# Sums over partitions in batches of eight steps through a ring of twelve products, and all fields gathered into one ring

## What is computed

```
e = jnp.stack([tbl_0[ids[:, 0]], ..., tbl_39[ids[:, 39]]], axis=1)      # 2048 x 40 x 64
vi, vj = e[:, i_idx, :], e[:, j_idx, :]                                  # 780 pairs i < j
viW = jnp.einsum('bpd,pde->bpe', vi, W)
z = jnp.einsum('bpe,bpe->bp', viW, vj)                                   # 2048 x 780
h = jnp.concatenate([z, dense_ctx], axis=1)
h = jnp.maximum(h @ W_top1 + b_top1, 0.0)                                # 796 -> 512
h = jnp.maximum(h @ W_top2 + b_top2, 0.0)                                # 512 -> 256
y = h @ W_top3                                                           # 256 -> 1
```

## Time and profile before

| | |
|---|---|
| median of 3 runs | 1378.1 us (1376.8 to 1378.47) |
| the profiled execution: its time | 1377.84 us |
| its span, first to last instruction | 1376.0 us |
| granted TensorE clock, mean | 0.994 |
| PE busy | 1305.7 us, 95% of the span, 7024 matmul records |
| DVE busy | 926.0 us, 67% |
| POOL busy | 605.2 us, 44% |
| ACT busy | 77.8 us, 6% |

### The profile page before, as it was taken

One profiled execution on the slowest core, in us unless ns is written; L12 is line 12 of the kernel. 1 busy time (PEld: TensorE's weight loads), 2 busy tenths in 40 slices (PEclk: granted clock), 3 DMA queues, 4 the chain that ended last, 5 costly groups with the idle time before them and its releaser, 6 DMA issues.

```text
span 1376.0 us, 16855 instructions
## 1 busy us (share of the span) xinstructions
PE 1305.7 (95%) x7024; PEld 463.0 (34%) x7024; DVE 926.0 (67%) x803; ACT 77.8 (6%) x97; POOL 605.2 (44%) x647
## 2 busy tenths in 40 slices
PE   1389999999999999999999999999999999999998
PEld 0133333333333333333333333333333333333333
DVE  0257888888656567787765666788776566788860
ACT  0000000000000000000000000000000000000001
POOL 6766443266754355766655456667660000000000
PEclk9989999999999999999999999999999999999999
DMA  4122221222222222222222223223221111111001
GB/s 151 26 62 62 57 70 52 68 61 65 82 54 68 66 72 75 62 82 63 63 59 82 63 66 87 61 62 83 63 62 52 52 54 52 53 44 54 1 1 42
DMA packets 36180, 84.43 MB, mean 61 GB/s; under 512 B 12420, under 2 KB 12420, under 8 KB 36104
## 3 DMA queue, kind: packets, MB, share of 16 engines
q1 hardware_dynamic: 11520, 52.43, 11.4%
q0 software_dynamic: 20560, 21.34, 7.9%
q10 hardware_dynamic: 4024, 9.58, 2.3%
HBM read 83.30 MB, written 0.01 MB: 61 GB/s over the span
## 4 chain that ended last, share of the span: by engine, by line
PE 92%; POOL 4%; issue 2%; DMA 1%; ACT 0%; DVE 0%; DVEq 0%; POOLq 0%
PE u L497 52%; PE zacc L512 27%; PE tacc L552 7%; PE u L471 3%; POOL gathered L312 2%; POOL first_fields L312 2%; PE tacc L555 2%; PE u L552 1%; DMA index<-ids 1%; PE u L555 1%; DMA gathered<-tbl,index 1%; PE tacc L559 1%; ACT h L369 0%; DVE prod L429 0%; DVEq L204 0%
## 5 line engine op out<-in xcount | busy, mean ns | idle before, releaser
L429 DVE TENSOR_TENSOR prod<-u,emb 128x1024 f32<-128x1024 f32 x800 | 925.8, 1216 | 409.2 <-PE u L497 409.2
L497 PE MATMUL u<-emb,weights 64*128 64x512 f32 x3200 | 753.6, 608 | 1.2 <-ACT emb L338 1.2
L312 POOL DMA_INDIRECT gathered<-tbl,index x512 | 482.9, 943 | 361.2 <-DVE prod L429 221.0
L497 PEld LDWEIGHTS u<-emb,weights 64*128 64x128 f32 x3200 | 291.6, 187 | 433.0 <-DVE prod L429 210.7
L512 PE MATMUL zacc<-prod,band 128*32 128x512 f32 x3200 | 391.7, 598 | 1.6 <-DVE prod L429 1.6
L512 PEld LDWEIGHTS zacc<-prod,band 128*32 128x32 f32 x3200 | 85.2, 109 | 278.9 <-DVE prod L429 147.9
L312 POOL DMA_INDIRECT first_fields<-tbl,index x128 | 120.8, 944 | 63.4 <-issue 32.6
L552 PE MATMUL tacc<-z,w12s 128*128 128x512 f32 (+1 forms) x196 | 97.4, 618 | 4.7 <-ACT h L369 4.7
L338 ACT ACTIVATE emb<-u 128x1024 f32<-128x1024 f32 x40 | 40.9, 1024 | 593.9 <-PE u L471 593.9
L552 PEld LDWEIGHTS tacc<-z,w12s 128*128 128x128 f32 (+1 forms) x196 | 33.2, 189 | 69.1 <-issue 59.5
L471 PE MATMUL u<-ident,first_fields 128*128 128x128 f32 x64 | 11.0, 318 | 43.4 <-DMA first_fields<-tbl,index 43.4
(11 more groups left out here) (17 smaller groups left out, 17.8 us busy)
## 6 DMA issues: line engine op xcount, KB each, us to landing
weights<-w_pairs SPq DMA_DIRECT2D x80, 640.0 KB
gathered<-tbl,index POOLq DMA_INDIRECT x512, 2.4
w12s<-w_top ACTq DMA_DIRECT2D x16, 448.0 KB, 3.3
first_fields<-tbl,index POOLq DMA_INDIRECT x128, 2.4
w12s<-w_top ACTq DMA_DIRECT2D x8, 256.0 KB, 2.5
index<-ids POOLq DMA_DIRECT2D x1, 320.0 KB, 7.2
z<-dense ACTq DMA_DIRECT2D x4, 32.0 KB, 1.8
y<-ysb ACTq DMA_DIRECT2D x4, 2.0 KB
```

The source lines that it names most:

```text
L312: pool.indirect_dma_start(out=to, out_offset=None, in_=tables[2 * t + e], in_offset=bass.IndirectOffsetOnAxis(ap=index[:, col:col + 1].bit ...
L429: nc.vector.tensor_tensor(prod[:, (c * len(COLUMNS) + m) % PRING, :, :], products, x, ALU.mult).then_inc(prod_ready, 1)
L497: last = nc.tensor.matmul(u[:, b, h, :], weights[half, w:w + P], x, start=True, stop=True)
```

## The change

Four things change in what runs. `SUMB` goes from 4 to 8 and `PRING` from 8 to 12. Behind each batch of sums there are now 4 matmuls of the network in layer 1 and 2 in layers 2 and 3. All 20 tiles of a chunk are gathered into the ring `gathered` of four places, and `first_fields` is gone. The code for rows is removed; it did not run.

```diff
-FT = 4
-FF = 2 * FT
-ROW_TILES = []
-
-SUMB = 4
-PRING = 8
+SUMB = 8
+PRING = 12
 LAG = 2
 UBUF = 3
 GRING = 4
...
                 elif tops:
-                    for _ in range(2 if tops[0][2][0] == 1 else 1):
+                    for _ in range(4 if tops[0][2][0] == 1 else 2):
                         if tops:
                             out.append(tops.pop(0))
...
-        first_fields = sb("first_fields", [P, 2, SUB, FF * DIM])
         gathered = sb("gathered", [P, GRING, SUB, P])
...
         def ring_use(c, t):
-            return (c * (T - FT) + t - FT) // GRING
+            return (c * T + t) // GRING
...
-                    if t < FT:
-                        if c >= 2 and ROWS and t == 0:
-
-                            pool.wait_ge(prod_ready, (c - 2) * N + ROWS[-1] + 1)
-                        if c >= 2:
-                            pool.wait_ge(rows_transposed, (c - 2) * TSTEPS + t // 2 + 1)
-                    elif ring_use(c, t):
-
-                        tile = c * (T - FT) + t - FT - GRING
-                        pool.wait_ge(rows_transposed,
-                                     tile // (T - FT) * TSTEPS + (tile % (T - FT) + FT) // 2 + 1)
+                    if ring_use(c, t):
+
+                        tile = c * T + t - GRING
+                        pool.wait_ge(rows_transposed, tile // T * TSTEPS + tile % T // 2 + 1)
                     for e in (0, 1):
                         if issue_step(c, 2 * t + e):

                             pool.wait_ge(prod_ready, issue_step(c, 2 * t + e))
```

More of the change, by code:

```diff
@@ L42, in make_steps @@
 def make_steps():
-    steps, units, n_units = [], [], 0
+    steps = []
     for t in range(T):
[L51 to L67, removed]
+        steps += [("col", k, t) for k in range(t)]
         if t % 2:
             steps.append(("half", t - 1))
-            units.append(n_units)
-            n_units += 1
-    return steps, units, n_units
+    return steps, list(range(len(steps))), len(steps)
 STEPS, UNITS, N_UNITS = make_steps()
@@ L78 @@
 assert WSLOTS * SLOT == N_UNITS and WSLOTS % WRING == 0
-COLUMNS = [n for n, s in enumerate(STEPS) if s[0] != "row"]
-ROWS = [n for n, s in enumerate(STEPS) if s[0] == "row"]
+COLUMNS = list(range(N))
 BATCHES = len(COLUMNS) // SUMB
@@ L127, in make_needs @@
     for n, s in enumerate(STEPS):
-        for t in ((s[1], s[2]) if s[0] == "col" else (s[1],) if s[0] == "row" else (s[1], s[1] + 1)):
+        for t in ((s[1], s[2]) if s[0] == "col" else (s[1], s[1] + 1)):
             needs.setdefault(t // 2, n)
@@ L155, in make_order @@
     tops = []
-    turns = []
     for c in range(CHUNKS):
@@ L161, in make_order @@
             out.append(("pairs", c, n))
[L162 to L167, removed]
             while sums and sums[0][0] * N + COLUMNS[sums[0][1] * SUMB + SUMB - 1] + LAG <= c * N + n:
@@ L175, in make_order @@
                 elif tops:
-                    for _ in range(2 if tops[0][2][0] == 1 else 1):
+                    for _ in range(4 if tops[0][2][0] == 1 else 2):
                         if tops:
                             out.append(tops.pop(0))
-    for _, c in turns:
-        out.append(("turn", c))
     for at, j in sums:
@@ L189 @@
 ORDER = make_order()
-USES = [o for o in ORDER if o[0] in ("pairs", "transpose", "turn")]
+USES = [o for o in ORDER if o[0] in ("pairs", "transpose")]
 BUFFER = {o: i % UBUF for i, o in enumerate(USES)}
 BEFORE = {o: USES[i - UBUF] if i >= UBUF else None for i, o in enumerate(USES)}
-Z_COPIES = [(o[1], o[2] if o[0] == "copy z" else ROW_BLOCK) for o in ORDER if o[0] in ("copy z", "turn")]
+Z_COPIES = [o[1:] for o in ORDER if o[0] == "copy z"]
 Z_COPY = {x: i + 1 for i, x in enumerate(Z_COPIES)}
@@ L406, in multiply @@
                 dve.wait_ge(u_ready, c * N + n + 1)
[L407 to L417, removed]
                 m = COLUMNS.index(n)
@@ L430, in multiply @@
                                         ).then_inc(prod_ready, 1)
[L432 to L441, removed]
             for o in ORDER:
@@ L456, in buffer_free @@
                     pe.wait_ge(prod_ready, last[1] * N + last[2] + 1)
-                elif last[0] == "transpose":
+                else:
                     pe.wait_ge(emb_ready, last[1] * TSTEPS + last[2] + 1)
-                else:
-                    pe.wait_ge(z_copied, Z_COPY[last[1], ROW_BLOCK])
             def transpose_step(c, i, b):
@@ L464, in transpose_step @@
                     t = 2 * i + h
[L465 to L468, removed]
+                    pe.wait_ge(rows_gathered[t % GRING], (ring_use(c, t) + 1) * 2 * SUB * 16)
                     for s in range(SUB):
-                        x = first_fields[:, c % 2, s, t * P:(t + 1) * P] if t < FT else gathered[:, (t - FT) % GRING, s, :]
-                        last = nc.tensor.transpose(u[:, b, h, s * P:(s + 1) * P], x, ident[:, :])
+                        last = nc.tensor.transpose(u[:, b, h, s * P:(s + 1) * P], gathered[:, t % GRING, s, :],
+                                                   ident[:, :])
                 last.then_inc(rows_transposed, 1)
@@ L483, in pair_step @@
                 base = c % 2 * T
-                t = step[2] if step[0] == "col" else step[1] if step[0] == "row" else step[1] + 1
+                t = step[2] if step[0] == "col" else step[1] + 1
                 if (c, "tile", t // 2) not in seen:
@@ L490, in pair_step @@
                     half = slice(h * DIM, (h + 1) * DIM)
[L491 to L497, removed]
+                    x = emb[half, base + step[1] + (h if step[0] == "half" else 0), :]
+                    last = nc.tensor.matmul(u[:, b, h, :], weights[half, w:w + P], x, start=True, stop=True)
                 last.then_inc(u_ready, 1)
@@ L515, in sum_step @@
                 last.then_inc(sums_done, 1)
[L517 to L521, removed]
             def top_step(c, item):
@@ L565, in _ @@
             for o in ORDER:
-                if o[0] in ("pairs", "transpose", "turn"):
+                if o[0] in ("pairs", "transpose"):
                     buffer_free(o)
@@ L573, in _ @@
                     sum_step(o[1], o[2])
-                elif o[0] == "turn":
-                    turn_rows(o[1], BUFFER[o])
                 elif o[0] == "top":
@@ L592, in z_rows @@
                 out += [(row + e, pair(2 * s[1] + h, 2 * s[2] + e)) for e in (0, 1)]
-    for r, t in enumerate(ROW_TILES):
-        for h in (0, 1):
-            out += [(ROW_BLOCK * P + r * 2 * FF + h * FF + f, pair(f, 2 * t + h)) for f in range(FF)]
     assert sorted(p for _, p in out) == list(range(PAIRS))
@@ L628 @@
                     w_pairs[1, :, at, :DIM] = own.T
-            elif step[0] == "col":
+            else:
                 for e in (0, 1):
                     w_pairs[h, :, at, e * DIM:(e + 1) * DIM] = w[pair(2 * step[1] + h, 2 * step[2] + e)]
-            else:
-                for f in range(FF):
-                    w_pairs[h, :, at + f // 2, f % 2 * DIM:(f % 2 + 1) * DIM] = w[pair(f, 2 * step[1] + h)].T
     w_pairs = given("w_pairs", w_pairs.reshape(P, WSLOTS, SLOT * P).transpose(1, 0, 2))
```

30 lines of the change are left out of this document (4 added, 26 removed).

## The result

| | before | after |
|---|---|---|
| median | 1377.47 us (4 runs) | 1430.53 us (1429.45 to 1431.24, 4 runs) |
| span of the profiled execution | 1376.0 us | 1428.8 us |
| ratio of the times | | 1.0384, 95% interval 1.0367 to 1.04 |

The change costs 53.1 us. The forecast was 1429, in a range of 1416 to 1443.

A forecast was written before the change was run, and what follows sets the result against it. PE was taken as the bound, with DVE slower inside a block. Blocks 55.3, last block +0.8, network -7.0 and +3.1, start -1.3 sum to 50.9 us; on 1377.84 that is 1428.7, said as 1429, range 1416 to 1443.

The forecast's parts named there:

- PE's time is the result's time: Whole kernel: PE is 95% busy and holds 92% of the last chain, so each microsecond it loses lengthens the result.
- The round of a plain block: Eight steps without transposition: DVE's pace delays the sums to 8.11 us, round 11.69 against 10.98, +0.71 us each.
- Fewer changes between kinds of matmul save 0.35 us a block: Steps and sums on PE: if nothing waits, 8 steps take 10.63 us where two rounds of 5.49 took 10.98.
- Blocks with a transposition: Transpositions within blocks: +0.15 us each for 23 after one to five steps, +0.54 for 9 after six or seven.
- The batch as a whole: Batches of 8: 55.3 us over the blocks, +0.8 for the last block, -1.3 hidden at the start.
- The start: Until 115.44 us PE is behind the gathers, so what blocks 1 and 3 lose is hidden: -1.3 us.
- Network, pieces and waits: Network matmuls: 36 fewer pieces at 0.195 us save 7.0 us; three more waits for ACT at 1.05 add 3.1.
- The last block: From step 195 of the chunk to the end of its sums: 13.41 us against 12.62, +0.8 us.
- The one ring for gathers: Gathers through one ring: no cost; the rival of late gathers said +10 to +27 us, chance 0.05.
- DVE's busy time: DVE over the profiled execution: still busy for 926 us.
- The clock: Rival: PE's new pauses lower the granted clock; one block in ten low gives +80 us, 1509 us; chance 0.03.

The follow-up runs named there:

- short products: The changed kernel with DVE multiplying only 384 of 512 samples of each step: 1543.04 us against 1520.98, and 1542.22 against 1516.44, for the kernel before.

## Why the prediction was right, point by point

The mechanism held. The terms that were off are the start and, by less, the network. The loss was forecast as 50.9 us and is 53.1. The time came nearer than that, 1429 against 1430.53, by a little luck: it was counted from 1378.1, and the kernel before has a median of 1377.47 with one run more.

- **PE's time is the result's time**: held. The loss sits in PE's blocks.
- **The round of a plain block**: forecast 8.11 to the sums and 11.69 in all; measured 8.11 and 11.68. The short products (7.07 us) show that it is DVE's pace, and the fact that both pieces of the network and transpositions shorten the wait shows that it is its backlog.
- **Fewer changes between kinds of matmul save 0.35 us a block**: held; with short products the round is 10.64 against 2 x 5.49 = 10.98.
- **Blocks with a transposition**: from the block to the sums, after three steps forecast 8.50, measured 8.52; after four 8.61 and 8.62 or 8.63; after six or seven 9.17 and 9.16 or 9.17. After one, two and five steps, which I had not walked, 9.06, 8.79 and 8.90. With the sums' 3.57 us these are +0.43, +0.15 and +0.26 against 12.20 before. Over all 23 blocks that is 3 x 0.43 + 3 x 0.15 + 6 x -0.12 + 8 x 0.19 + 3 x 0.26 = 3.3 us, where I took 3.5.
- **The batch as a whole**: 55.3 + 0.8 - 1.3 = 54.8 forecast, 56.2 measured.
- **The start**: this term is the largest miss. It said that the gathers hide what the first blocks lose (the -1.3; the two blocks it names come one right behind the other). But PE reaches the step that follows the last wait for a gather at 115.82 us (116.03 before), and the next block at 123.03 (121.52 before). So 1.5 us are lost by then, where the prediction's terms leave 0.15. The lines below show why: before, 8 sums stood ahead of that wait and 8 behind it; after, all 16 stand behind, where no wait hides them.
- **Network, pieces and waits**: -7.0 + 3.1 = -3.9 forecast, -3.1 measured, together with the one ring (forecast 0). Between the traces of the two kernels the rounds with a piece gain 2.9 us over rounds without one. The nine waits are there, at 1.05 us: 4.68 against 3.63. The pieces taken away saved less than 0.195 us each: before, one with a transposition right behind it took 1.82 us (745.24 to 747.06), not 1.91.
- **The last block**: 13.41 forecast, 13.38 measured.
- **The one ring for gathers**: no wait of PE for a gather after 120 us. POOL waits once for its ring, 7.5 us, as before with 6.8. The last wait for a gather is 0.67 us at 115.23, not 1.57 at 115.44 as forecast.
- **DVE's busy time**: forecast as before, 926 us; measured 917.8. Eight products in one piece take 9.14 us, two pieces of four 9.24.
- **The clock**: 1.00 from 100 to 1420 us. The pauses inside the blocks did not bring it down; that rival was given 0.03.

PE around the last wait for a gather, first in the kernel before, then in the kernel after:

```profile
111.37 1.92 PE L512 MATMUL zacc<-prod,band 128*32 128x512 f32 x16
...
119.67 1.92 PE L512 MATMUL zacc<-prod,band 128*32 128x512 f32 x16
121.52 2.85 PE L497 MATMUL u<-emb,weights 64*128 64x512 f32 x12
```

```profile
115.23 0.66 PE L380 MATMUL u<-ident,gathered 128*128 128x128 f32 x4 [0.67 <-DMA gathered<-tbl,index]
115.82 3.70 PE L402 MATMUL u<-emb,weights 64*128 64x512 f32 x16
119.45 3.64 PE L417 MATMUL zacc<-prod,band 128*32 128x512 f32 x32
```

The one ring wait of the kernel after:

```profile
POOL gathered L258 <- PE u L380: 7.5, 1, 7.5
```

## What to carry to other kernels

Two engines in a pipeline can be busy for 95% and 64% of the span, and the second still be what holds the first up: compare their pace *inside* the stretch in which both run. Here a step costs PE 0.855 us and DVE 1.133 us. Three buffers hide that for four steps and not for eight, and each further step of a batch costs the difference. A longer batch saves its change of kind of matmul (0.35 us) only as far as the buffers reach. Put work that needs nothing of the slower engine into the middle of the stretch, not at its end, and cut such work where its own groups end.

## What the runs showed of the hardware

On chip A the kernel before took 1521 us (1511.99 to 1530.18, 17 runs), on chip B 1516 us (1509.48 to 1524.96, 17 runs), on the others 1377. The trace of the run with the one ring alone, on chip A, shows what differs. Most blocks are as fast as elsewhere: 125 of 160 undivided blocks of 4 steps take 3.63 or 3.64 us. The 35 others take up to 11.57. A product is no longer than elsewhere (1218 ns in the mean, 1216 before). PE's waits for products from 118 to 1490 us in that run, of which the kernel before has one on the other chips, at the very end:

```profile
PE u L402 <- DVE prod L357: 53.9, 20, 6.7
PE u L402 <- issue: 17.0, 12, 3.1
...
PE zacc L417 <- DVE prod L357: 7.3, 8, 1.7
```

and one place of it:

```profile
649.08 1.99 PE L402 MATMUL u<-emb,weights 64*128 64x512 f32 x8
...
651.02 1.02 ACT L284 ACTIVATE emb<-u 128x1024 f32<-128x1024 f32 x1 [27.56 <-remote]
...
652.49 1.23 DVE L357 TENSOR_TENSOR prod<-u,emb 128x1024 f32<-128x1024 f32 x1 [2.75 <-PE u L402]
```

PE's step begins at 649.08, so DVE could have begun 1.18 us later, at 650.26. It begins at 652.49. DVE and ACT begin such work some us late now and then, and with three buffers of `u` PE then stops.

The granted clock falls as well. The stretches of this run up to POOL's last gather and behind it, and then the first of them in the kernel before, with the clock third from the end:

```profile
118.00:1186.00 1068.00, 967.15 (x5128) 331.40 (x5122) 680.58 (x586) 57.63 (x70) 535.50 (x568) 0.96 0.21 59
1186.00:1450.00 264.00, 262.44 (x1398) 89.26 (x1396) 189.70 (x165) 8.72 (x13) 0.33 (x1) 1.00 0.14 47
```

```profile
118.00:1186.00 1068.00, 1063.33 (x5799) 375.59 (x5799) 765.87 (x663) 63.08 (x78) 524.42 (x556) 1.00 0.24 65
```

In the first stretch the clock goes to its lower level, 1.2 GHz, 14 times; the fall at 1006.9 us, for one, comes right behind a wait of PE of 4.0 us. By the clock of 0.96 that costs about 0.04 x 1068 = 43 us, an estimate, of the 155 us by which this execution's span is longer than that of the kernel before. The waits of PE from 118 to 1490 us add up to 102 us, where the kernel before has 6.3 us of waits behind 118 us; a part of the 155 us lies before 118 us.

All of this stops when POOL has done its gathers. In each of the seven runs on these chips 52 to 79 products behind 118 us begin over 0.5 us late (counted from the end of the product before or from 1.18 us after the step's start, whichever is later). The last of them begins at 1159 to 1188 us, by run; POOL issues its last gather at 1184 to 1204 us. That ties the delays to the time of the gathers and not yet to the gathers themselves: from 225 to 315 us POOL gathers too, and no product is late. What holds DVE and ACT on those chips stays open. The kernel after was not run there.

A reader should take from it that a few tenths of a per cent gained on one chip (0.9977 for the larger pieces, the one ring and the ring of twelve) can be a loss on another (1.0117 and 1.0134).
